# Threshold search with counts in each engine's own unit, and the spread's root taken from the variance's bits on VectorE

## The reference

```python
Q = (h @ Wq.T); K = (h @ Wk.T)                      # 4 heads of 32, summed over heads
sim = einsum('bhnd,bhmd->bnm', Q, K) / (sqrt(32) * 4)
k = int(512 * 0.3)                                  # 153
threshold = top_k(sim, k)[0][:, :, -1:]             # the 153rd largest of each row of 512
A = sigmoid(sim) * (sim >= threshold)
A = (A + swap(A)) * 0.5
x = x + tanh(g_xattn) * ((1 - gamma) * layernorm(x) + gamma * A)
x = x + tanh(g_ffn) * moe(layernorm(x))             # 8 experts, top 2, silu(x w1) * (x w3), then w2
```

## Time and profile before

| | us |
|---|---|
| median of 3 runs | 771.75 |
| lowest and highest of them | 769.46, 771.84 |
| the profiled execution's own time | 769.46 |
| its span in the profile | 767.7 |
| PE busy in it | 719.1 |
| VectorE busy in it | 398.1 |
| ScalarE busy in it | 332.6 |
| GpSimd busy in it | 200.5 |

### The profile page before, as it was taken

How to read it: one execution, slowest core, us unless ns; L and a number is a source line. 1 busy time by engine, 2 the same in 40 slices (tenths; PEclk the granted TensorE clock), 3 DMA queues, 4 the chain that set the end, 5 groups by cost and what they waited for, 6 DMA issues and landing times.

```text
span 767.7 us, 13122 instructions
## 1 busy us (share of the span) xinstructions
PE 719.1 (94%) x4507; PEld 620.1 (81%) x4509; DVE 398.1 (52%) x1013; ACT 332.6 (43%) x649; POOL 200.5 (26%) x243
## 2 busy tenths in 40 slices
PE   7698798795999999999999999999999999999994
PEld 3494443574989998999989989999999899989993
DVE  2787779884554355425443564254535542644312
ACT  4797485512454244333533353335333533544221
POOL 4203824972204110403030304030403040203111
PEclk9758999998999999999999999999999999999997
DMA  8972253417516340543226324432363244303122
GB/s 311 411 302 111 110 220 115 138 15 282 178 80 199 121 112 33 135 160 69 109 58 236 69 109 121 166 74 104 62 232 69 109 138 152 67 1 69 42 27 28
DMA packets 24231, 98.76 MB, mean 129 GB/s; under 512 B 4560, under 2 KB 4816, under 8 KB 20368
## 3 DMA queue, kind: packets, MB, share of 16 engines
q1 hardware_dynamic: 14496, 70.54, 23.9%
q0 software_dynamic: 9568, 27.96, 16.1%
q10 hardware_dynamic: 144, 0.00, 0.0%
HBM read 77.50 MB, written 20.99 MB: 128 GB/s over the span
## 4 chain that ended last, share of the span: by engine, by line
issue 67%; POOL 11%; DVE 8%; PE 7%; POOLq 3%; DMA 2%; DVEq 1%; ACT 1%; SPq 0%
POOL x_body L528 4%; POOL out L534 4%; DVE front L1204 2%; POOL xb L474 2%; PE bank L627 1%; PE bank L674 1%; DMA out<-xb 1%; PE bank L600 1%; POOLq L542 1%; PE bank L683 1%; POOLq L331 1%; DVE scratch L1179 1%; PE bank L672 1%; PE bank L590 1%; DMA front<-ctxT 1%
## 5 line engine op out<-in xcount | busy, mean ns | idle before, releaser
L729 PE MATMUL bank<-xT_body_hi,w_hi 128*128 128x256 f32 (+1 forms) x960 | 275.8, 287 | 3.9 <-issue 3.6
L731 PE MATMUL bank<-xT_body_lo,w_hi 128*128 128x256 f32 (+1 forms) x960 | 275.3, 287 | 0.8 <-issue 0.8
L730 PE MATMUL bank<-xT_body_hi,w_lo 128*128 128x256 f32 (+1 forms) x960 | 275.1, 287 | 0.0
L729 PEld LDWEIGHTS bank<-xT_body_hi,w_hi 128*128 128x128 f32 x960 | 181.1, 189 | 10.7 <-issue 5.4
L730 PEld LDWEIGHTS bank<-xT_body_hi,w_lo 128*128 128x128 f32 x960 | 181.5, 189 | 3.6
L731 PEld LDWEIGHTS bank<-xT_body_lo,w_hi 128*128 128x128 f32 x960 | 181.2, 189 | 0.0
L1735 DVE TENSOR_TENSOR h<-bank,act_g 128x256 f32<-128x256 f32 (+1 forms) x120 | 52.4, 437 | 207.5 <-PE bank L731 202.2
L1116 ACT ACTIVATE hT_hi<-h 128x256 fp32r<-128x256 f32 (+1 forms) x120 | 51.4, 428 | 165.6 <-DVE h L1735 165.6
L1369 DVE TENSOR_TENSOR w_lo<-raw,w_hi 128x1024 fp32r<-128x1024 f32 x88 | 105.2, 1223 | 25.0 <-ACT w_hi L958 25.0
L1112 ACT ACTIVATE act_g<-bank 128x256 f32<-128x256 f32 (+1 forms) x120 | 46.5, 388 | 162.2 <-PE bank L731 162.0
L729 PE MATMUL bank<-w_hi,hT_hi 128*128 128x512 f32 (+1 forms) x280 | 114.1, 408 | 1.9 <-DVE hT_lo L1648 1.8
(11 more groups left out here) (307 smaller groups left out, 772.1 us busy)
## 6 DMA issues: line engine op xcount, KB each, us to landing
raw<-weights SPq DMA_DIRECT2D x24, 2048.0 KB, 10.4
raw<-xT SPq DMA_DIRECT2D x4, 1024.0 KB, 11.6
xb<-x SPq DMA_DIRECT2D x4, 1024.0 KB, 20.2
w_hi<-weights POOLq DMA_DIRECT2D x2, 2048.0 KB, 14.9
found<-xb SPq DMA_DIRECT2D x4, 1024.0 KB, 4.5
out<-xb SPq DMA_DIRECT2D x4, 1024.0 KB, 6.9
found<-scratch SPq DMA_DIRECT2D x1, 2092.0 KB, 30.2
front<-ctxT SPq DMA_DIRECT2D x4, 256.0 KB, 4.6
```

What stands on the lines that cost most here:

```text
L729: nc.tensor.matmul(out_ap, hi, hi_w, start=start, stop=False)
L730: nc.tensor.matmul(out_ap, lo, hi_w, start=False, stop=False)
L731: return nc.tensor.matmul(out_ap, hi, lo_w, start=False, stop=stop)
```

## The change

Three things are rewritten, all on the search.

1. The count stays in the unit in which each engine has it. ScalarE's accumulator goes straight into the probe pair (as 512 minus twice the count), VectorE counts the elements below the probe (512 minus the count) instead of those at or above it. The conversion L1210 goes. The constants that a count is compared with (`KTH`, `AIM`, the start values of low and high, the slope's factor) become small rows with three values in VectorE's unit and five in ScalarE's. Operations with a constant become operations with such a row.
2. VectorE takes the root itself: the variance's bits, shifted right by one and with a constant added, read as a float again. GpSimd's two power operations and the semaphore `sd_set` go; GpSimd issues the two weight transfers as soon as the second half's moments are there.
3. The first step is prepared in `first_probes` (`step`), and `next_probes` has one small subtraction more (`low_over`).

```diff
-                nc.gpsimd.tensor_tensor(sim_sd[:, ts], sim_mv[:, ts, 1], half_pow[:, ts], ALU.pow).then_inc(sd_set, 1)
+            pool.wait_ge(sim_moments, 2)
...
-                                                bias=probe[k % 2][:, t, 0:1], scale=-1.0, accum_out=act_sum[:, t:t + 1])
+                                                bias=probe[k % 2][:, t, 0:1], scale=-1.0, accum_out=probe[k % 2][:, t, 1:2])
...
-            V.memset(low[:, :, 1], 296.6)
-            V.memset(high[:, :, 1], 58.9)
+            def unit(row, count):
+                V.memset(row[:, 0:ON_VECTOR], N - count)
+                V.memset(row[:, ON_VECTOR:HALF], N - 2 * count)
+            for half in range(2):
+                ts = slice(half * HALF, (half + 1) * HALF)
+                unit(low[:, ts, 1], 296.6)
+                unit(high[:, ts, 1], 58.9)
+            unit(kth_row, float(KTH))
+            unit(aim_row, AIM)
+            V.memset(slope_row[:, 0:ON_VECTOR], 1.0 / NEWTON)
+            V.memset(slope_row[:, ON_VECTOR:HALF], 0.5 / NEWTON)
...
             def first_probes(half):
-                dve.wait_ge(sd_set, half + 1)
+                dve.drain()
+                V.tensor_single_scalar(sim_sd_i[:, ts], sim_mv[:, ts, 1].bitcast(I32), 1, ALU.logical_shift_right)
+                dve.drain()
+                V.tensor_single_scalar(sim_sd_i[:, ts], sim_sd_i[:, ts], ROOT, ALU.add)
+                dve.drain()
...
-                V.tensor_scalar(slope[:, ts], sim_sd[:, ts], 1.0 / NEWTON, None, ALU.mult)
+                V.tensor_tensor(slope[:, ts], sim_sd[:, ts], slope_row, ALU.mult)
+                dve.drain()
+                V.tensor_tensor(step[:, ts], slope[:, ts], aim_row, ALU.mult)
+                dve.drain()
+                V.tensor_tensor(step[:, ts], probe[0][:, ts, 0], step[:, ts], ALU.add)
                 dve.drain()
...
-                    V.tensor_scalar(flags[n], S[:, t, :], probe[k % 2][:, t, 0:1], None, ALU.is_ge, ALU.add,
+                    V.tensor_scalar(flags[n], S[:, t, :], probe[k % 2][:, t, 0:1], None, ALU.is_lt, ALU.add,
...
             def all_counts(half, k):
                 dve.wait_ge(act_counted[half], k + 1)
-                at = slice(half * HALF + ON_VECTOR, (half + 1) * HALF)
-                V.tensor_scalar(probe[k % 2][:, at, 1], act_sum[:, at], -0.5, N / 2.0, ALU.mult, ALU.add)
                 dve.drain()
...
-                V.tensor_scalar(is_low[:, :, :], counts, float(KTH), None, ALU.is_ge)
-                V.tensor_scalar(is_high[:, :, :], counts, float(KTH), None, ALU.is_lt)
+                V.tensor_tensor(is_low[:, :, :], counts, least, ALU.is_le)
+                V.tensor_tensor(is_high[:, :, :], counts, least, ALU.is_gt)
...
-                V.scalar_tensor_tensor(frac[:, :], probe[0][:, ts, 1], -AIM, slope[:, ts], ALU.add, ALU.mult)
-                dve.drain()
-                V.tensor_tensor(probe[1][:, ts, 0], probe[0][:, ts, 0], frac[:, :], ALU.add).then_inc(probe_set[half], 1)
+                V.tensor_tensor(frac[:, :], probe[0][:, ts, 1], slope[:, ts], ALU.mult)
+                dve.drain()
+                V.tensor_tensor(probe[1][:, ts, 0], step[:, ts], frac[:, :], ALU.subtract).then_inc(probe_set[half], 1)
...
                 V.tensor_tensor(span[:, :, :], low[:, ts, :], high[:, ts, :], ALU.subtract)
+                V.tensor_tensor(low_over[:, :], low[:, ts, 1], aim_row, ALU.subtract)
                 dve.drain()
                 V.reciprocal(inv[:, :], span[:, :, 1])
                 dve.drain()
-                V.scalar_tensor_tensor(frac[:, :], low[:, ts, 1], -AIM, inv[:, :], ALU.add, ALU.mult)
+                V.tensor_tensor(frac[:, :], low_over[:, :], inv[:, :], ALU.mult)
...
-            V.tensor_scalar(in_window[:, :], high[:, :, 1], float(KTH - WINDOW), None, ALU.is_ge)
+            near = units[:, 1, :]
+            unit(near, float(KTH - WINDOW))
+            dve.drain()
+            V.tensor_tensor(in_window[:, :].rearrange("p (h t) -> p h t", h=2), high[:, :, 1].rearrange("p (h t) -> p h t", h=2),
+                            near.unsqueeze(1).to_broadcast([P, 2, HALF]), ALU.is_le)
```

More of the change, by code:

```diff
@@ L58 @@
 NEWTON = 180.5
+ROOT = 0x1FBD1DF5
 BIG = 3.0e38
@@ L144, in build @@
         sim_sd = sb("sim_sd", [P, TILES], F32, part1)
-        half_pow = sb("half_pow", [P, TILES], F32, part1)
         rsqrt_pow = sb("rsqrt_pow", [P, TB], F32, part1)
@@ L150, in build @@
         slope = sb("slope", [P, TILES], F32, part1)
+        step = sb("step", [P, TILES], F32, part1)
         inv = sb("inv", [P, HALF], F32, part1)
+        low_over = sb("low_over", [P, HALF], F32, part1)
         act_sum = sb("act_sum", [P, TILES], F32, part1)
+        sim_sd_i = sim_sd[:, :].bitcast(I32)
+        units = sb("units", [P, 3, HALF], F32, part1)
+        kth_row, aim_row, slope_row = (units[:, k, :] for k in range(3))
         is_low = sb("is_low", [P, HALF, 2], I32, part1)
@@ L291, in build @@
         qk_mm, qk_out, sim_mm, sim_out = sem("qk_mm"), sem("qk_out"), sem("sim_mm"), sem("sim_out")
-        sim_moments, sd_set = sem("sim_moments"), sem("sd_set")
+        sim_moments = sem("sim_moments")
         probe_set = [sem("probe_set0"), sem("probe_set1")]
@@ L391, in _ @@
         def _(pool):
-            nc.gpsimd.memset(half_pow[:, :], 0.5)
             nc.gpsimd.memset(rsqrt_pow[:, :], -0.5)
@@ L435, in _ @@
             pool.dma_start(more_pads, pads[:, 1:3, :]).then_inc(more_pads_in, 16)
-            for half in range(2):
-                ts = slice(half * HALF, (half + 1) * HALF)
-                pool.wait_ge(sim_moments, half + 1)
-                nc.gpsimd.tensor_tensor(sim_sd[:, ts], sim_mv[:, ts, 1], half_pow[:, ts], ALU.pow).then_inc(sd_set, 1)
+            pool.wait_ge(sim_moments, 2)
             for q in range(2):
@@ L1217, in tighten @@
                 counts = now[:, ts, 1:2].to_broadcast([P, HALF, 2])
-                V.tensor_scalar(is_low[:, :, :], counts, float(KTH), None, ALU.is_ge)
-                V.tensor_scalar(is_high[:, :, :], counts, float(KTH), None, ALU.is_lt)
+                least = kth_row.unsqueeze(2).to_broadcast([P, HALF, 2])
+                V.tensor_tensor(is_low[:, :, :], counts, least, ALU.is_le)
+                V.tensor_tensor(is_high[:, :, :], counts, least, ALU.is_gt)
                 dve.drain()
```

## The result

The changed kernel takes 819.68 us (median of 4 runs, 818.69 to 822.72) against 771.66 (4 runs, 769.46 to 771.84) before: 1.0633 times as long, 95% interval 1.0613 to 1.0652. That is 48 us slower, where a gain of 1.65 was forecast.

What follows compares the result with a forecast made beforehand. PE, busy 719.1 of 767.7 us in the experts' loop, was taken as the bound. In the search 1.45 + 0.16 + 0 - 0.05 = 1.56 us, taken as 1.65, against 771.75 gave 770.1 us, range 767.5 to 772.3.

Steps and rivals of the forecast that it cites:

- the first one: Experts' loop: PE busy 719.1 of 767.7 us there, untouched by the change, so only the search stage was to be read.
- the exact pass: Rival, chance 0.02: root too rough, a row's threshold falls outside the eight, the pass runs for all tiles, about 1,260 us.
- the search's start: VectorE's first probes at about 21.3 and 30.4, gate_c near 31.4, L616 near 31.7 and 27.45 us long.
- The 14 small memsets ... cost nothing: At VectorE's begin, ahead of 4 us of waiting for the gains: no cost; without that cover some 0.8 us.
- The root: In `first_probes`, on VectorE in place of GpSimd's power: first probe 1.23 us earlier in one half, 1.18 in the other.
- the step: Behind the slope in `first_probes`: two more drained instructions, 0.25 us each, cost 0.50 us per half.
- the conversion: L1210 removed: 0.08 us less per half and round, 0.16 gained in `second_probes`, spent again on `low_over` in six later rounds.
- the swap: Comparisons with a row in place of a constant, some 18 on the path: 0 to 0.18 us lost, taken as 0.05.
- The later rounds: VectorE's six later search rounds: still 4.20 us each, the removed conversion and the added `low_over` cancelling.
- The stall: Rival, chance 0.19: the unexplained 0.53 us before L1229 goes too, 0.45 more gained, 2.1 us in all, 769.7 us.
- Two-input spacing: Rival, chance 0.09: undrained two-input pairs on VectorE 0.17 us apart, not 0.08; 1.26 us lost, 771.4 us.
- Does the saved time arrive?: From search to end: gain passed on in full; rival, chance 0.10, PE's clock eats the 1.65 us, 771 to 772.5.

Runs made afterwards that it cites:

- b31_idle_code: The kernel before with 31 drains added in a branch that isn't taken: 823.03 us (4 runs), ratio 1.0677.
- a97_timed: The changed kernel with 97 drains in the branch that isn't taken, timed in 6 runs: 767.89 us, ratio 0.9957 to the kernel before.
- a225_idle_code: The changed kernel with 225 drains in the branch that isn't taken, a shift of 256: 772.9 us (10 runs), ratio 1.0019.
- root_only_118: The kernel before with only the root taken from the bits on VectorE, and 118 idle drains: 769.11 us (10 runs), ratio 0.9977.
- units_only_107: The changed kernel with GpSimd's two powers and `sd_set` put back, and 107 idle drains: 770.95 us (10 runs), ratio 1.0005.
- b31_run_code: The kernel before with 31 drains executed at VectorE's begin, where it waits for the gains: 822.03 us.
- a97_idle_code: The changed kernel with 97 drains in the branch that isn't taken, a shift of 128, run once: 770.02 us.
- best_80: The changed kernel without `step` and without the drain at the end of `next_probes`, with 80 idle drains: 768.50 us (6 runs), ratio 0.9965.

## Why the prediction was wrong

**The step that failed** is the first one: "That is the experts' loop, which the change doesn't touch, so the total says nothing about this edit". I wrote it of the total in the earlier trace rows, and left the loop out of every later step. The change doesn't touch the loop's operations, but it moves their place in VectorE's code, and that was worth 48 us. The wait that the forecast had at nothing, at the loop's head, went from 20.5 to 107.3 us. `b31_idle_code` has the loss with nothing of the change in it, `a97_timed` and `a225_idle_code` have the change without the loss. No rival covered it. The only one for a large loss was another mechanism, the exact pass, and its instructions are not in the trace. Counted from the first moments, the search's start came as forecast: the probes 1.2 and 10.3 us behind them, gate_c 11.3, L617 (L616 before) 11.6 and 27.45 us long, ScalarE's wait of 2.00 gone.

It could have been asked beforehand. The earlier trace rows had a stall of 0.53 us in front of L1229 "in which it waits for nothing shown", the waits of before had 20.5 us of the same kind at the head of 15 bodies, and its page had a queue of instructions. I took the first for a matter of 0.45 us and didn't ask for the other two.

**"The 14 small memsets ... cost nothing"** holds for their time. They are instructions all the same, 12 more than before, and so 12 of the 31.

**The root** was forecast at -1.23 and -1.18 us, and another -0.08 for L1197: 2.49. `root_only_118` gained 1.76 with two stalls (0.51, and 0.44 at L1246) in place of one of 0.53, and a new wait of 0.19 for ScalarE's copy: 1.76 + 0.42 + 0.19 = 2.37, so the term was right within 0.12. The addition on integers, not in the trace of before, starts its follower 0.25 us later, as taken.

**The units and the step** were forecast at +1.00 for the step, -0.16 for the conversion, +0.05 for the swap: +0.89. `units_only_107` lost 1.04, with stalls of 0.50, and 0.36 at L1257, in place of one of 0.53: 1.04 - 0.33 = 0.71. The two together make 2.37 - 0.71 = 1.66, where the sum had 1.65. The later rounds are at 4.20 us as forecast.

**The stall** (the rival with 0.19): it went, and the search gained 2.06 in place of 1.65: 1.66 and the 0.45. Neither reason that I gave was the right one. It belongs to a place in the code: counted from VectorE's first instruction, with each accumulator read as one, L1229 before, L1193 in `root_only_118`, L1187 in `units_only_107` and L1179 in `b31_run_code` are all number 64, the first being number 0. Further stalls are at 192 (L1246 in `root_only_118`), 576 and 704, or one or two places behind: 128 apart, or a multiple of it. In the four kernels just named number 63 is a drain. In the changed kernel it is an accumulator read, 64 and 192 follow flags of 0.74 us with no drain between, and no gap shows at either. That this is why its stall went is read from the traces, and no run tests it. That L1229's fell under GpSimd's issue was chance: in `units_only_107` the issue is where it was, and the stall isn't.

**Two-input spacing** (0.09): refuted, 0.09 us at L1238 to L1239 and at L1259 to L1260, against 0.08 for one input.

**Does the saved time arrive?** That isn't settled. With the same search, shorter by 2.0 to 2.1 us, `a97_timed` is 3.1 us faster than the kernel before and `a225_idle_code` 1.8 us slower; its loop stands as well. Part of these 5 us is the price of the idle code itself. The first instruction behind the branch that isn't taken, in the kernel before, `a97_timed` and `a225_idle_code`:

```profile
87.63 0.06 DVE L1339 MEMSET small<- 128x1 f32 x1 [1.24 <-issue]
...
85.65 0.06 DVE L1366 MEMSET small<- 128x1 f32 x1 [1.60 <-issue]
...
88.33 0.06 DVE L1366 MEMSET small<- 128x1 f32 x1 [3.98 <-issue]
```

With up to 118 idle this gap is 1.2 to 1.7 us, with 128 and 225 it is 3.86 and 3.98, so the longer jump costs some 2.4 us. The other 2.6 stay open. In `a97_idle_code`'s one execution the search ended 2.0 us ahead, but its first `weight_body` came at 193.44 us against 193.53. In between, PE's granted clock was 0.93 against 1.00 from 100 to 150 us, and GpSimd waited for a transfer for 11.3 in place of 10.0 us; which of them took the gain isn't shown. Why `a97_timed`'s gain is 1.0 us more than its search's, and why `best_80`'s further 1.06 doesn't show, stays open too. So does why a long gap is 10 us when a piece is 8.3 KB.

## What to carry to other kernels

In a program with a loop on the device, every instruction ahead of the loop, executed or not, moves it; compare the packets of the instruction queue and the "issue" gap at the loop's head before believing that a change elsewhere made a loop slower, or that it can't. If they jump, pad with code in a branch that is never taken and time again; only then is the change itself being measured. Pad with as little as does it: 128 and 225 idle made the jump over them 2.4 us longer, up to 118 didn't. For an outermost loop of B instructions on VectorE, with B from 257 to 384, these runs suggest 384 - B + 1 good places of 128, and no bad one for a shorter loop; neither was tried with another B.

## What the runs showed of the hardware

- VectorE's code comes in pieces of 128 instructions (8.3 KB a packet). A loop of 326 is slow where it touches four of them: 8.4 to 11.4 us at each jump back of the outer loop, 2.3 to 7.4 us at those of the inner, and at a shift of 16, where only the outer touches four, 0.19 at those of the inner (0.47 at the last).
- Going straight on over the edge of a piece stalls VectorE by 0.36 to 0.53 us where a drain stands at it; no gap shows in the changed kernel, where two edges lie among flags of 0.74 us.
- A jump forward over code that isn't run takes 1.2 to 1.7 us with up to 118 idle instructions more in it, and 3.9 to 4.0 with 128 or 225.
- Instructions that are never executed count for the place of the loop and of the stalls.
- A root from a float's bits, two drained integer operations of 128x8 on VectorE, is done 1.24 us after the moments' start (0.64 of which are the moments), where GpSimd's power held it for 2.45.
